# Two of three row blocks direct, a third of the pairs partly through products of transformed rows: a 3x3 convolution with group normalisation

## Chip, core and metric

One core of one Trainium2 chip. The metric is the device time of one execution in microseconds, the median of several runs. Five engines work in parallel, each in the order of its own queue: TensorE (PE, with its weight loads PEld), VectorE (DVE), ScalarE (ACT), GpSimd (POOL) and SyncE (SP), which issues all DMA transfers here. They are ordered against each other by semaphores alone.

## What is computed

```python
# x: 32 images of 64 channels, 56 x 56, float32; W: 64 x 64 x 3 x 3
bw = sign(W)                                   # value of clip(W) + (sign(W) - clip(W))
g = x.reshape(32, 32, 2, 56, 56)               # 32 groups of two channels
n = (g - mean(g)) / sqrt(var(g) + 1e-5)        # over the two channels and all pixels
out = x + conv(n.reshape(x.shape), bw, padding=1)
```

## The kernel before

Two images make a **pair**: their 2 x 64 channels fill the 128 partitions. There are 16 pairs. A pair's x lies in one of eight slots of `xbuf` and receives the result in place. x is normalised (times 512) into an upper half and a lower half, both float16, in `halves`; the products of both with the signs are summed in float32.

**TensorE** (L388 to L447) works in four quadrants of 64 x 64. Two of them, "home", put an image's rows into the PSUM partitions of its own image; the other two, "away", put them into the other image's partitions. A phase has 7 rows of each stream: first nine taps on the upper half, then nine on the lower. One tap of one stream is a *step* of two matmuls. A pair has four phases, two per group of 28 rows, and a PSUM bank for each block; banks alternate by group, so that group e waits until the results of group e-2 have been taken out. Before its nine lower taps a phase waits for POOL's lower half of the rows that it reads (`wait_lower`). Before the first pair, 14 rounds of matmuls on constants (L393) run while the data arrive, then the weights are turned by matmuls (L401) and copied out of PSUM by ACT (L272, L273).

**DVE** (L291 to L386), for pair k: adds the home rows of the group before to x (`add_home`, L345), takes seven statistics of pair k+2 (`pair_stats`, L302), adds home and away rows of the pair's first group (L345, L353), then makes the coefficients of pair k+2 (`coefficients`, L304 to L324), in which ACT takes a square root.

**ACT** (L236 to L289), for pair k: moves the away rows of the second group of pair k-2 out of PSUM (`move_away`, L268), waits for the coefficients of k, writes upper halves and the float32 normalised values by chunks of rows (L258, L250), takes the square root for k+1 (L245).

**POOL** (L205 to L234), for pair k: adds the rows that ACT moved for pair k-2 to x (`add_away`, L225), then subtracts upper halves from the normalised values to make the lower halves, chunk by chunk (`lo`, L216). Pairs 0 and 1 have four chunks, later ones two (rows 0 to 28 and 29 to 55). POOL and ACT thus prepare pair k while TensorE computes pair k-1.

**SP** (L160 to L203) stores a group once its home and away rows are added, and loads pieces of pair k+4 as phases of pair k end.

## Time and profile before

| | us |
|---|---|
| median of 3 runs | 209.88 (209.35 to 210.86) |
| the profiled execution | 210.1 |
| its span, first to last instruction | 208.3 |
| busy in the span: PE, DVE, ACT, POOL | 197.3, 154.3, 136.4, 128.4 |

The profile is one execution. Its page gives busy times, a chain of work followed back from the last instruction, and groups of instructions by line. The trace behind it gives instructions in order of time, with what ended the idle time before them. Durations of matmuls are modelled at their ends; their starts and the waits of other engines for them show TensorE's pace.

### The profile page before, as it was taken

To read this page: it belongs to the slowest core of one execution; us is meant where nothing else is said; L and a number is where in the kernel's file an instruction comes from. 1 tells how busy PE (TensorE), PEld (TensorE's weight loads), DVE (VectorE), ACT (ScalarE), POOL (GpSimd) and SP (SyncE) were. 2 spreads that over 40 slices of the span, in tenths; PEclk is the share of its full clock that TensorE was granted. 3 is DMA by queue.
4 is the path that set the end of the run, shared out by engine and by line. 5 is a ranking of instruction groups with operands and counts; after the bars stand their busy time and mean duration, and the time that the engine had idled before them with its cause. 6 is when DMAs were issued, how large, how long until landed. Compare 5 with 4: busy or idle time off the path is not lost.

```text
span 208.3 us, 10333 instructions
## 1 busy us (share of the span) xinstructions
PE 197.3 (95%) x4754; PEld 178.2 (86%) x4754; DVE 154.3 (74%) x317; ACT 136.4 (65%) x122; POOL 128.4 (62%) x56
## 2 busy tenths in 40 slices
PE   0979999999999999999999999999999999999990
PEld 0568898989898898989888898989888999999990
DVE  1897999987777887777778887777778787534092
ACT  3187979784939486693939587593939678492100
POOL 1026867975775939575784948576693957577300
PEclk9979999999999999999999999999999999999999
DMA  6999657999696967979686968968696334434345
GB/s 223 366 401 358 227 163 235 342 309 335 216 323 227 312 200 266 340 232 344 231 321 220 318 223 301 321 230 311 235 318 208 146 116 157 159 157 157 129 150 190
DMA packets 18699, 52.19 MB, mean 251 GB/s; under 512 B 2080, under 2 KB 4384, under 8 KB 18656
## 3 DMA queue, kind: packets, MB, share of 16 engines
q1 hardware_dynamic: 18656, 51.54, 69.9%
q8 instruction: 37, 0.61, 1.1%
q14 instruction: 6, 0.05, 0.1%
HBM read 25.84 MB, written 25.69 MB: 247 GB/s over the span
## 4 chain that ended last, share of the span: by engine, by line
PE 92%; DVE 3%; DMA 2%; ACT 1%; issue 0%; DVEq 0%
PE psum L444 89%; PE psum L395 3%; DMA xbuf<-in_x_dram 2%; DVE xbuf L365 1%; DVE xbuf L353 1%; DVE xbuf L345 0%; PE psum L401 0%; DVE xbuf L361 0%; ACT halves L258 0%; ACT w_taps L272 0%; DVEq L95 0%; ACT w_taps L273 0%
## 5 line engine op out<-in xcount | busy, mean ns | idle before, releaser
L444 PE MATMUL psum<-halves,w_taps 64*64 64x385 f16 (+5 forms) x4680 | 191.1, 324 | 1.5 <-ACT halves L258 1.5
L444 PEld LDWEIGHTS psum<-halves,w_taps 64*64 64x64 f16 x4680 | 174.6, 108 | 17.9 <-ACT w_taps L273 1.6
L216 POOL TENSOR_TENSOR halves<-xnorm,halves 128x1624 f16<-128x1624 f32 (+4 forms) x35 | 100.0, 2872 | 37.1 <-ACT xnorm L250 36.8
L302 DVE BATCH_NORM_STATS2 stats<-xbuf 128x6 f32<-128x448 f32 x112 | 60.6, 613 | 3.7 <-DMA xbuf<-in_x_dram 3.6
L345 DVE SCALAR_TENSOR_TENSOR xbuf<-psum,xbuf 128x784 f32<-128x784 f32 x31 | 30.2, 974 | 38.2 <-PE psum L444 38.2
L258 ACT ACTIVATE halves<-xbuf,coef 128x1624 f16<-128x1624 f32 (+5 forms) x36 | 55.1, 1534 | 1.3 <-DVE coef L323 1.0
L250 ACT ACTIVATE xnorm<-xbuf,coef 128x1624 f32<-128x1624 f32 (+4 forms) x35 | 54.2, 1549 | 0.0
L225 POOL TENSOR_TENSOR xbuf<-xbuf,moved 128x784 f32<-128x784 f32 x15 | 27.9, 1860 | 29.1 <-ACT moved L268 29.1
L268 ACT ACTIVATE moved<-psum 64x784 f32<-64x784 f32 x30 | 24.6, 819 | 25.0 <-PE psum L444 24.6
L353 DVE SCALAR_TENSOR_TENSOR xbuf<-psum,xbuf 64x784 f32<-64x784 f32 x32 | 31.1, 973 | 1.0
L245 ACT ACTIVATE std<-own,eps 128x1 f32<-128x1 f32 x16 | 4.7, 295 | 22.6 <-DVE own L312 22.6
L395 PE MATMUL psum<-filler 64*64 64x448 f16 x56 | 5.3, 565 | 4.7 <-DMA xbuf<-in_x_dram 4.7
L312 DVE BATCH_NORM_AGGREGATE own<-stats 128x2 f32<-128x84 f32 x16 | 8.5, 534 | 0.6
L395 PEld LDWEIGHTS psum<-filler 64*64 64x64 f16 x56 | 2.4, 168 | 7.0 <-DMA xbuf<-in_x_dram 4.7
L241 ACT ACTIVATE w_sign<-w_raw 64x576 f16<-64x576 f32 x1 | 0.7, 682 | 6.4 <-DMA w_raw<-in_L_conv_W_dram 6.4
L319 DVE TENSOR_SCALAR dev<-var,inv,std 128x1 f32<-128x1 f32 x16 | 4.4, 273 | 0.6
L317 DVE RECIPROCAL inv<-std 128x1 f32<-128x1 f32 x16 | 2.6, 164 | 2.8 <-ACT std L245 2.8
L323 DVE TENSOR_SCALAR coef<-own,coef 128x1 f32<-128x1 f32 x16 | 3.4, 214 | 0.6
L309 DVE STREAM_SHUFFLE stats<-stats 128x42 f32<-128x42 f32 x16 | 3.2, 203 | 0.5
L321 DVE RECIPROCAL coef<-dev 128x1 f32<-128x1 f32 x16 | 2.6, 164 | 0.5
L314 DVE TENSOR_SCALAR var<-own 128x1 f32<-128x1 f32 x16 | 2.5, 154 | 0.6
L365 DVE SCALAR_TENSOR_TENSOR xbuf<-psum,xbuf 64x392 f32<-64x392 f32 (+2 forms) x6 | 2.6, 427 | 0.2
(19 smaller groups left out, 9.6 us busy)
## 6 DMA issues: line engine op xcount, KB each, us to landing
out_dram<-xbuf SPq DMA_DIRECT2D x63, 392.0 KB, 3.3
xbuf<-in_x_dram SPq DMA_DIRECT2D x48, 448.0 KB, 5.4
xbuf<-in_x_dram SPq DMA_DIRECT2D x16, 224.0 KB, 4.6
out_dram<-xbuf SPq DMA_DIRECT2D x1, 224.0 KB, 2.7
out_dram<-xbuf SPq DMA_DIRECT2D x1, 168.0 KB, 3.0
w_raw<-in_L_conv_W_dram SPq DMA_DIRECT2D x1, 144.0 KB, 6.1
```

The costliest lines, as they stand in the source:

```text
L216: nc.gpsimd.tensor_tensor(at(halves[:, k % HRING, 1, :], a, b), at(xnorm[:, k % NRING, :], a, b), at(halves[:, k % HRING, 0, :], a, b), AL ...
L225: nc.gpsimd.tensor_tensor(away, away, moved[:, m % 2], ALU.add).then_inc(add_done, 1)
L245: nc.scalar.activation(std[:], own[:, 1:2], ACT.Sqrt, bias=eps[:], scale=QUARTER).then_inc(std_ready, 1)
L250: nc.scalar.activation(at(xnorm[:, k % NRING, :], a, b), at(xbuf[:, s, :], a, b), ACT.Identity, bias=coef[:, s, 1:2], scale=coef[:, s, 0:1 ...
L258: nc.scalar.activation(at(halves[:, k % HRING, 0, :], a, b), at(xbuf[:, s, :], a, b), ACT.Identity, bias=coef[:, s, 1:2], scale=coef[:, s, ...
L268: nc.scalar.mul(moved[here, m % 2], psum[there, bank:bank + 2, 0:BN], 1.0 / SCALE).then_inc(move_done, 1)
L302: nc.vector.bn_stats(stats[:, n, :], xbuf[:, s, a:b]).then_inc(blocks_ready, 1)
L312: nc.vector.bn_aggr(own[:], stats[:]).then_inc(var_ready, 1)
L345: nc.vector.scalar_tensor_tensor(rows, psum[:, bank:bank + 2, 0:BN], 1.0 / SCALE, rows, ALU.mult, ALU.add).then_inc(home_done, 1)
L353: nc.vector.scalar_tensor_tensor(rows[here], psum[there, bank:bank + 2, 0:BN], 1.0 / SCALE, rows[here], ALU.mult, ALU.add).then_inc(away_d ...
L395: pe.matmul(psum[cols, 3 + 4 * (n // 2), 0:448], filler[lanes, 0:CO], filler[lanes, :], start=True, stop=True)
L444: mm = pe.matmul(outs[:, r0 - first:r1 - first, left:right], w_taps[lanes, t, :], ins[:, :, left + dx:right + dx], start=(half == 0 and n ...
```

## The change

In five of the sixteen pairs (2, 5, 8, 11, 14) the home stream computes rows 25 to 42, nine pairs of rows, through four products per two rows in place of six: from the rows above, odd, even and below, POOL makes differences and sums of x (`make_lines`: STEP = even - odd, DIFF of rows two apart, SUM = odd + even), ACT and DVE make their upper and lower halves (`line_upper`, `line_lower`, and POOL's `lo_sums`), and TensorE multiplies each of the four (9 x 56 = 504 columns) by three weights, sums and differences of the taps, that POOL makes once (`weights_of_products`). The first two products are scaled and combined with x by DVE (`turn`), added and subtracted by POOL (`cross`), and added to the last two by DVE into `xbuf` (`finish`). The other 13 home rows and 25 away rows of such a pair stay direct, in blocks of 7 and 6, and of 8, 8 and 9 rows. Both away units of such a pair are moved by ACT and added by POOL (before, DVE added the first). The lower and upper halves of rows 26 to 41 are not made for them.

Home and away have separate counters of finished blocks, and TensorE's order is made step by step: the stream with fewer columns so far goes next. The chain of coefficients is cut into `aggregate`, at the end of DVE's round, and `scale`, at the start of the next, with a third coefficient for the sums. At the start there are 11 rounds on constants instead of 14 and 7 more after the weights are turned; the weights are copied out in three parts, two of them after the first upper half.

```diff
 AHEAD = 4
-WARM_UP = 14
+WARM_UP = 11
+KEEP_WARM = 7
+
+
+
+
+
+WINOGRAD = (2, 5, 8, 11, 14)
...
+    WROW, WROWS = 25, 18
+    WPAIRS = WROWS // 2
+    WN = WPAIRS * W
+
+    def home_units(k):
+        if k == LAST:
+            return [[(0, 7), (14, 7)], [(28, 7), (42, 4)], [(50, 3)]]
+        if k in WINOGRAD:
+            return [[(WROW + WROWS, 7), (WROW + WROWS + 7, 6)], [2, 1], [0, 3]]
+        return [[(0, 7), (14, 7)], [(28, 7), (42, 7)]]
+
+    def away_units(k):
+        if k == LAST:
+            return [[(7, 7), (21, 7)], [(35, 7), (46, 4)], [(53, 3)]]
+        if k in WINOGRAD:
+            return [[(0, 8), (8, 8)], [(16, 9)]]
+        return [[(7, 7), (21, 7)], [(35, 7), (49, 7)]]
...
+    def by_scalar(k, i):
+
+        return k != LAST and (i == 1 or k in WINOGRAD)
...
+        if k in WINOGRAD:
+            return [(0, 26), (42, 56)]
...
+            def store_unit(k, i):
+                if k in WINOGRAD:
+                    if i == 0:
+                        wait_away(k, 0)
+                        store(k, 0, 16)
+                        sp.wait_ge(home_done, home_before(k) + 1)
+                        store(k, WROW + WROWS, H)
+                    else:
+                        wait_away(k, 1)
+                        store(k, 16, WROW)
+                        sp.wait_ge(home_done, home_before(k) + 3)
+                        store(k, WROW, WROW + WROWS)
+                    return
...
+                        sp.wait_ge(away_conv, away_blocks_before(k) + min(n, 3))
...
+            def make_lines(k):
+                s = k % XRING
+                for n in (1, 2):
+                    pool.wait_ge(loaded[s][n], landed(k))
+                if winograd_before(k):
+
+                    before = WINOGRAD[winograd_before(k) - 1]
+                    pool.wait_ge(home_done, home_before(before) + 2)
+                    pool.wait_ge(line_lo_ready, winograd_before(k))
+                    pool.wait_ge(sums_norm_ready, winograd_before(k))
+                pairs_of_rows = at(xbuf[:, s, :], WROW, WROW + WROWS).rearrange("p (r m) -> p r m", m=2 * W)
+                odd, even = pairs_of_rows[:, :, 0:W], pairs_of_rows[:, :, W:]
+                nc.gpsimd.tensor_tensor(lines[:, STEP].rearrange("p (r w) -> p r w", w=W), even, odd,
+                                        ALU.subtract).then_inc(lines_made, 1)
+                nc.gpsimd.tensor_tensor(lines[:, DIFF], at(xbuf[:, s, :], WROW - 1, WROW + WROWS - 1),
+                                        at(xbuf[:, s, :], WROW + 1, WROW + WROWS + 1), ALU.subtract).then_inc(lines_made, 1)
+                nc.gpsimd.tensor_tensor(lines[:, SUM].rearrange("p (r w) -> p r w", w=W), odd, even,
+                                        ALU.add).then_inc(lines_made, 1)
...
+            def lo_sums(k):
+                n = winograd_before(k)
+                pool.wait_ge(sums_norm_ready, n + 1)
+                pool.wait_ge(line_hi_ready, 2 * (n + 1))
+                nc.gpsimd.tensor_tensor(line_halves[:, 1, SUM], sums_norm[:], line_halves[:, 0, SUM],
+                                        ALU.subtract).then_inc(sums_lo_ready, 1)
+
+            def cross(k):
+                n = winograd_before(k)
...
+                nc.gpsimd.tensor_tensor(crossings[:, 0], turns[:, 0], turns[:, 1], ALU.add).then_inc(crossed, 1)
+                nc.gpsimd.tensor_tensor(crossings[:, 1], turns[:, 0], turns[:, 1], ALU.subtract).then_inc(crossed, 1)
+
+            def weights_of_products():
+                pool.wait_ge(w_ready, KH)
+                middle, above, below = (w_taps[:, n] for n in range(KH))
+                nc.gpsimd.tensor_tensor(w_outer[:], above, below, ALU.add).then_inc(outer_ready, 1)
+                nc.gpsimd.tensor_scalar(w_products[:, 0], above, 1.0 / SCALE, 0.0, ALU.mult, ALU.add).then_inc(products_ready, 1)
+                nc.gpsimd.tensor_scalar(w_products[:, 3], below, -1.0 / SCALE, 0.0, ALU.mult, ALU.add).then_inc(products_ready, 1)
+                pool.wait_ge(outer_ready, 1)
+                nc.gpsimd.tensor_tensor(w_products[:, 1], w_outer[:], middle, ALU.add).then_inc(products_ready, 1)
+                nc.gpsimd.tensor_tensor(w_products[:, 2], w_outer[:], middle, ALU.subtract).then_inc(products_ready, 1)
...
             for k in range(NP):
 
                 if k >= 2:
-                    add_away(2 * (k - 2) + 1)
+                    if k - 2 in WINOGRAD:
+                        cross(k - 2)
+                    add_away(k - 2, 1)
+                if k in WINOGRAD:
+                    make_lines(k)
                 for c in range(len(chunks(k))):
                     if (k, c) != (0, 0):
                         lo(k, c)
-            add_away(LAST - 2)
+                if k in WINOGRAD:
+                    lo_sums(k)
+                if k - 1 in WINOGRAD:
+                    add_away(k - 1, 0)
+                if k == 1:
+                    weights_of_products()
+            if LAST - 1 in WINOGRAD:
+                cross(LAST - 1)
+            add_away(LAST - 1, 1)
...
+                unit = away_units(k)[i]
+                size = unit[0][1] * W
                 for here, there in ((LOW, HIGH), (HIGH, LOW)):
-                    nc.scalar.mul(moved[here, m % 2], psum[there, bank:bank + 2, 0:BN], 1.0 / SCALE).then_inc(move_done, 1)
+                    nc.scalar.mul(moved[here, m % 2, 0:len(unit) * size].rearrange("p (n m) -> p n m", m=size),
+                                  psum[there, bank:bank + len(unit), 0:size], 1.0 / SCALE).then_inc(move_done, 1)
...
+            def line_upper(k):
...
+                act.wait_ge(lines_made, 3 * n + 2)
...
+                nc.scalar.activation(line_halves[:, 0, 0:3 * WN], lines[:, 0:3 * WN], ACT.Identity,
+                                     scale=coef[:, s, 0:1]).then_inc(line_hi_ready, 1)
+                act.wait_ge(lines_made, 3 * n + 3)
...
+                                     bias=coef[:, s, 2:3], scale=coef[:, s, 0:1]).then_inc(line_hi_ready, 1)
...
+                nc.scalar.activation(sums_norm[:], lines[:, SUM], ACT.Identity,
+                                     bias=coef[:, s, 2:3], scale=coef[:, s, 0:1]).then_inc(sums_norm_ready, 1)
...
             act.wait_ge(w_turned, 1)
-            nc.scalar.copy(w_taps[:, 0:8, :], psum[:, 0, :].rearrange("p (t o) -> p t o", o=CO)).then_inc(w_ready, 1)
-            nc.scalar.copy(w_taps[:, 8, :], psum[:, 1, 0:CO]).then_inc(w_ready, 1)
+            w_copy(0)
...
+                    if (k, c) == (0, 0):
+                        w_copy(1)
+                        w_copy(2)
+                    else:
                         normalise(k, c)
+                if k in WINOGRAD:
+                    line_upper(k)
                 if k + 1 < NP:
                     deviation(k + 1)
-            move_away(LAST - 2)
+                if k - 1 in WINOGRAD:
+                    move_away(k - 1, 0)
+            move_away(LAST - 1, 1)
...
+            def scale(k):
...
+                nc.vector.tensor_scalar(coef[:, s, 2:3], own[:, 0:1], -2.0, coef[:, s, 0:1],
                                         ALU.mult, ALU.mult).then_inc(coef_ready, 1)
...
+                if k in WINOGRAD:
+                    (first, rows), (second, fewer) = home_units(k)[i]
+                    add_rows(k, bank, first, rows)
+                    add_rows(k, bank + 1, second, fewer).then_inc(home_done, 1)
+                    return
...
+            def line_lower(k):
+                n = winograd_before(k)
+                dve.wait_ge(line_hi_ready, 2 * n + 1)
...
+            def turn(k):
...
+                dve.wait_ge(home_conv, home_blocks_before(k, 1) + 1)
+                dve.wait_ge(lines_made, 3 * (n + 1))
+                nc.vector.scalar_tensor_tensor(turns[:, 1], psum[:, bank, 0:WN], 1.0 / SCALE, lines[:, STEP],
+                                               ALU.mult, ALU.subtract).then_inc(turned, 1)
+                dve.wait_ge(home_conv, home_blocks_before(k, 1) + 2)
+                nc.vector.scalar_tensor_tensor(turns[:, 0], psum[:, bank + 1, 0:WN], 1.0 / SCALE, lines[:, SUM],
                                                ALU.mult, ALU.add).then_inc(home_done, 1)
...
+            def finish(k):
...
+                dve.wait_ge(crossed, 2 * (n + 1))
+                dve.wait_ge(home_conv, home_blocks_before(k, 3))
+                for j in range(2):
+                    row = nc.vector.scalar_tensor_tensor(
+                        pairs_of_rows[:, :, j * W:(j + 1) * W], crossings[:, j].rearrange("p (r w) -> p r w", w=W), 0.5,
+                        psum[:, bank + j, 0:WN].rearrange("p (r w) -> p r w", w=W), ALU.mult, ALU.add)
+                row.then_inc(home_done, 1)
...
             for k in range(NP):
 
-                if k >= 1:
-                    add_home(2 * k - 1)
+                if 1 <= k < NP - 1:
+                    scale(k + 1)
+                if k >= 1 and k - 1 not in WINOGRAD:
+                    add_home(k - 1, 1)
                 if 1 <= k < NP - 2:
-                    pair_stats(k + 2)
-                add_home(2 * k)
-                add_away(2 * k)
+                    pair_stats(k + 2, range(4))
+                if k - 1 in WINOGRAD:
+                    finish(k - 1)
+                if 1 <= k < NP - 2:
+                    pair_stats(k + 2, range(4, NSTAT))
+                add_home(k, 0)
+                if k not in WINOGRAD:
+                    add_away(k, 0)
                 if k == 0:
-                    pair_stats(2)
+                    pair_stats(2, range(NSTAT))
                 if k < NP - 2:
-                    coefficients(k + 2)
-            for n, p in enumerate(phases[phases_before(LAST):]):
-                add_phase(p, n)
+                    aggregate(k + 2)
+                if k + 1 in WINOGRAD:
+                    line_lower(k + 1)
+                if k in WINOGRAD:
+                    turn(k)
...
+            warm(KEEP_WARM)
...
+            def wait_bank(b):
+
+                if b.unit < 2:
+                    return
+                if not b.away:
+                    pe.wait_ge(home_done, b.unit - 1)
+                elif by_scalar(*AWAY[b.unit - 2]):
+                    pe.wait_ge(move_done, 2 * moves_before(b.unit - 1))
+                else:
+                    pe.wait_ge(away_done, 2 * aways_before(b.unit - 1))
...
+            def wait_lower(b):
+                k = b.pair
+                if b.product == 1:
+                    pe.wait_ge(sums_lo_ready, winograd_before(k) + 1)
+                elif b.product is not None:
+                    pe.wait_ge(line_lo_ready, winograd_before(k) + 1)
...
+            for k in range(NP):
+                home, away = blocks_of(k, False), blocks_of(k, True)
+
+                home_time = away_time = 0
+                h = a = home_step = away_step = 0
+                while h < len(home) or a < len(away):
+                    if h < len(home) and (a == len(away) or home_time <= away_time):
+                        step(home[h], home_step)
+                        home_time += columns(home[h])
+                        h, home_step = (h, home_step + 1) if home_step + 1 < 2 * home[h].halfway else (h + 1, 0)
+                    else:
+                        step(away[a], away_step)
+                        away_time += columns(away[a])
+                        a, away_step = (a, away_step + 1) if away_step + 1 < 2 * away[a].halfway else (a + 1, 0)
```

## Rows read from the trace of the kernel before

**Rows 1.** The page: busy time by engine; the chain's shares by line.

```profile
PE 197.3 (95%) x4754; PEld 178.2 (86%) x4754; DVE 154.3 (74%) x317; ACT 136.4 (65%) x122; POOL 128.4 (62%) x56
...
PE psum L444 89%; PE psum L395 3%; DMA xbuf<-in_x_dram 2%; DVE xbuf L365 1%; DVE xbuf L353 1%; DVE xbuf L345 0%; PE psum L401 0%; DVE xbuf L361 0%; ACT halves L258 0%; ACT w_taps L272 0%; DVEq L95 0%; ACT w_taps L273 0%
```

**Rows 2.** Timeline, one steady pair: start, duration (us), engine, line, operation, [idle before <-releaser].

```profile
85.30 0.97 DVE L345 SCALAR_TENSOR_TENSOR xbuf<-psum,xbuf 128x784 f32<-128x784 f32 x1 [0.77 <-PE psum L444]
85.30 1.66 ACT L268 ACTIVATE moved<-psum 64x784 f32<-64x784 f32 x2 [1.72 <-PE psum L444]
...
86.99 1.75 ACT L258 ACTIVATE halves<-xbuf,coef 128x1624 f16<-128x1624 f32 x1
87.04 1.87 POOL L225 TENSOR_TENSOR xbuf<-xbuf,moved 128x784 f32<-128x784 f32 x1 [2.11 <-ACT moved L268]
...
90.44 6.31 POOL L216 TENSOR_TENSOR halves<-xnorm,halves 128x1624 f16<-128x1624 f32 x2 [1.53 <-ACT xnorm L250]
91.28 0.98 DVE L345 SCALAR_TENSOR_TENSOR xbuf<-psum,xbuf 128x784 f32<-128x784 f32 x1 [1.31 <-PE psum L444]
91.81 1.63 ACT L250 ACTIVATE xnorm<-xbuf,coef 128x1512 f32<-128x1512 f32 x1
92.29 1.98 DVE L353 SCALAR_TENSOR_TENSOR xbuf<-psum,xbuf 64x784 f32<-64x784 f32 x2
...
95.11 0.15 DVE L314 TENSOR_SCALAR var<-own 128x1 f32<-128x1 f32 x1
...
96.14 0.21 DVE L323 TENSOR_SCALAR coef<-own,coef 128x1 f32<-128x1 f32 x1
97.12 1.67 ACT L268 ACTIVATE moved<-psum 64x784 f32<-64x784 f32 x2 [1.72 <-PE psum L444]
```

**Rows 3.** Groups by shape: line, engine, operation, shapes, count | busy us, mean ns.

```profile
L216 POOL TENSOR_TENSOR halves<-xnorm,halves 128x1624 f16<-128x1624 f32 x14 | 46.0, 3288 | 21.6 <-ACT xnorm L250 21.6
L216 POOL TENSOR_TENSOR halves<-xnorm,halves 128x784 f16<-128x784 f32 x4 | 6.7, 1680 | 13.4 <-ACT xnorm L250 13.3
L225 POOL TENSOR_TENSOR xbuf<-xbuf,moved 128x784 f32<-128x784 f32 x15 | 27.9, 1860 | 29.1 <-ACT moved L268 29.1
L209 POOL TENSOR_SCALAR_AFFINE_SELECT ident<-ident 64x64 f16<-64x64 f16 x1 | 0.2, 234 | 0.2 <-POOL ident L207 0.2
L337 DVE TENSOR_TENSOR halves<-xnorm,halves 128x840 f16<-128x840 f32 x1 | 1.0, 1034 | 0.3 <-ACT halves L258 0.3
L361 DVE SCALAR_TENSOR_TENSOR xbuf<-psum,xbuf 128x392 f32<-128x392 f32 x1 | 0.6, 567 | 0.0
```

**Rows 4.** Timeline, columns as before: the startup, pair 2's preparation, the last pair.

```profile
12.46 1.03 DVE L337 TENSOR_TENSOR halves<-xnorm,halves 128x840 f16<-128x840 f32 x1 [0.30 <-ACT halves L258]
12.46 9.85 PE L444 MATMUL psum<-halves,w_taps 64*64 64x392 f16 x193 [1.50 <-ACT halves L258]
14.30 1.68 POOL L216 TENSOR_TENSOR halves<-xnorm,halves 128x784 f16<-128x784 f32 x1 [12.95 <-ACT xnorm L250]
...
25.19 3.34 POOL L216 TENSOR_TENSOR halves<-xnorm,halves 128x784 f16<-128x784 f32 x2 [0.18 <-ACT xnorm L250]
...
33.47 6.32 POOL L216 TENSOR_TENSOR halves<-xnorm,halves 128x1624 f16<-128x1624 f32 x2 [1.54 <-ACT xnorm L250]
...
38.02 1.66 ACT L268 ACTIVATE moved<-psum 64x784 f32<-64x784 f32 x2 [0.17 <-PE psum L444]
...
197.66 0.98 DVE L345 SCALAR_TENSOR_TENSOR xbuf<-psum,xbuf 128x784 f32<-128x784 f32 x1 [4.94 <-PE psum L444]
```

**Rows 5.** Windows, TensorE: stretch, length, busy (instructions), granted clock, DMA.

```profile
11.00:12.40 1.40, 0.00 (x0) 1.00 1.05 406
13.00:13.50 0.50, 0.50 (x14) 0.62 1.10 430
13.50:16.00 2.50, 2.50 (x38) 0.50 1.02 396
16.00:17.00 1.00, 1.00 (x26) 0.74 1.04 404
```

More of the change, by code:

```diff
@@ L53, in conv_preact_kernel @@
     NP = B // 2
-    LAST = 2 * NP - 1
-    phases = []
-    for e in range(2 * NP):
-        first = 28 * (e % 2)
-        here = 2 * (e % 2)
-        if e < LAST:
-            cuts = [(first, 7, here), (first + 14, 7, here + 1)]
-        else:
-            cuts = [(first, 7, here), (first + 14, 4, here + 1), (first + 22, 3, (here + 2) % 4)]
-        phases += [Phase(e // 2, e, row, n, bank, 4 + bank) for row, n, bank in cuts]
-    def phases_before(e):
-        return 2 * e + (e > LAST)
-    def by_scalar(e):
-        return e % 2 == 1 and e != LAST
@@ new lines, in away_blocks_before, with blocks_of @@
+    def away_blocks_before(k, i=0):
+        return (sum(len(u) for j in range(k) for u in away_units(j))
+                + sum(len(u) for u in away_units(k)[:i]) if k < NP else sum(len(u) for j in range(k) for u in away_units(j)))
+    def blocks_of(k, away):
+        out = []
+        for i, unit in enumerate(away_units(k) if away else home_units(k)):
+            u = (away_before(k) if away else home_before(k)) + i
+            for j, what in enumerate(unit):
+                bank = 2 * (u % 2) + j + (4 if away else 0)
+                if isinstance(what, int):
+                    out.append(Block(k, u, bank, away, WROW, WROWS, what))
+                else:
+                    out.append(Block(k, u, bank, away, *what))
+        return out
@@ L189, in _ @@
                 if k >= 1:
-                    store_group(2 * k - 1)
+                    store_unit(k - 1, 1)
                 if XRING <= k + AHEAD < NP:
@@ L356, in add_phase, with add_rows @@
[L356 to L366 removed]
+            def add_rows(k, bank, first, rows):
+                part = at(xbuf[:, k % XRING, :], first, first + rows)
+                return nc.vector.scalar_tensor_tensor(part, psum[:, bank, 0:rows * W], 1.0 / SCALE, part, ALU.mult, ALU.add)
@@ new lines, in add_last @@
+            def add_last(n, home, away):
+                dve.wait_ge(home_conv, home_blocks_before(LAST, 1) + n + 1)
+                add_rows(LAST, home.bank, home.first, home.rows).then_inc(home_done, 1)
+                dve.wait_ge(away_conv, away_blocks_before(LAST, 1) + n + 1)
+                part = at(xbuf[:, LAST % XRING, :], away.first, away.first + away.rows)
+                for here, there in ((LOW, HIGH), (HIGH, LOW)):
+                    nc.vector.scalar_tensor_tensor(part[here], psum[there, away.bank, 0:away.rows * W], 1.0 / SCALE,
+                                                   part[here], ALU.mult, ALU.add).then_inc(away_done, 1)
@@ L368, in _ @@
             for k in range(2):
-                pair_stats(k)
-                coefficients(k)
+                pair_stats(k, range(NSTAT))
+                aggregate(k)
+                scale(k)
                 if k == 0:
@@ new lines, in _, with last_chunk @@
+            mm.then_inc(w_turned, 1)
+            warm(KEEP_WARM)
[6 more added lines that the diff above has]
+                    pe.wait_ge(move_done, 2 * moves_before(b.unit - 1))
+                else:
+                    pe.wait_ge(away_done, 2 * aways_before(b.unit - 1))
+            def last_chunk(b):
+                k = b.pair
+                return next(n for n, (a, z) in enumerate(chunks(k)) if min(b.first + b.rows, H - 1) < z)
```

301 lines of the change are left out of this document (191 added, 110 removed).

## The prediction

> **What bounds the kernel now.** I read the page first. TensorE is busy 95% of the span and one matmul line is 89% of the chain that ended last; every other engine is below 75% [rows 1]. So time is made or lost on TensorE only, and the question is which other engine would become late for it. The timeline of one steady pair answers that [rows 2]. A pair takes 97.12 - 85.30 = 11.82 us, its first half 91.28 - 85.30 = 5.98 us for 36 steps (18 taps for each of two blocks), 166 ns a step; the second half takes 5.84 us. The 0.14 us between them are the six steps in which one stream lacks the image's edge row: each of the two streams (home, away) goes at its own pace, and a step is priced by its columns: 392 cost 166 ns, so 336 cost 142, 448 cost 190, 504 cost 214.
>
> Write T for the moment at which a pair starts on TensorE (85.30). Then ACT moves the last away rows from T to T+1.7, writes the next pair's halves, and its last normalised chunk ends at T+8.1 (91.81 + 1.63). POOL adds the moved rows T+1.7 to T+3.6, idles, starts the next pair's lower halves at T+5.14 and is done at T+11.45, with only 0.4 us of the pair left. DVE's last coefficient is ready at T+11.05. POOL is nominally 62% busy, but its work lies late in the pair: that is the engine to watch.
>
> **Startup before.** The pair of index 2 starts at 38.0 (ACT's move, released by TensorE) and POOL's halves for it run 33.47 to 39.8 [rows 4]. TensorE stood still from 11.0 to 12.4; its granted clock then fell to 0.5, the lower of its two levels (1.2 of 2.4 GHz), from about 13.1 to 16.5 by the fractions 0.62 and 0.74 [rows 5]: 3.4 us at half, 1.7 us lost.
>
> **The change: TensorE.** In pairs 2, 5, 8, 11, 14 ("W pairs") the home stream has 24 steps of 504 columns (5.13 us), 18 of 392 (2.99) and 18 of 336 (2.56), less 0.14 at the edge: 10.54 us. Away: 36 of 448 (6.83), less 0.14, and 18 of 504 (3.85): 10.54 us. A W pair saves 11.82 - 10.54 = 1.28 us; five save **6.4 us**. All else must be hidden to keep it.
>
> **Prices on POOL.** Its lower halves cost 3.288 us for 1624 elements, 1.680 for 784; its add of two f32 operands 1.860 for 784, so 2.37 ns an element [rows 3]. The new operations are such adds; I take 2.37, with 2.02 (3288/1624) as the low end. make_lines has 2016 elements: 4.78 us (low 4.07). cross has 1008: 2.39 (2.04). The add of 896 moved elements: 2.13 (1.81). Chunks of 1456 and 784: 2.97 between the two measured sizes, and 1.68; lo_sums 1.08. The five weight operations of 192 f16 elements: 0.46 each, 2.3 (low, by the 0.234 of a 64x64 operation: 1.2; high, on the line through the lower halves: 2.7).
>
> **First W pair (pair 2).** Before, POOL finishes pair 1's halves at 25.19 + 3.34 = 28.53 [rows 4]. The third coefficient adds one 0.21 us instruction before them: 28.8. Then in POOL's queue: weights 2.3, pair 0's add 1.86 (its move ends before that), make_lines 4.78, the two chunks 4.65: **42.4** (low 40.6, high 42.8). TensorE may start pair 2 by 36.1, two pairs after 12.4, but reaches the lower half of its first block after 9 steps, 1.5 us, and stands until 42.4. All of it is thus as late as if it had started at 40.9: **+2.9 us** against 38.0 (1.1 to 3.3). The longer fill, the weights copied in three parts and the earlier start are worth nothing to the end, since POOL's chain, not TensorE's, sets 42.4; that chain starts at the coefficients. If the wait were gone, they would bring up to 2 us.
>
> Standing still for some 4.8 us costs clock: 1.4 us did before. I take the same **+1.7 us** (0.5 to 2.5, as the trace has this event once).
>
> **Later W pairs, their start.** POOL, from T-11.82: add until T-8.21, lines until T-3.43, chunks until T+1.22, needed at T+1.5: 0, with 0.3 us of cover. ACT's three line_upper operations (1512, 504, 504 elements; 1624 take 1.75) fit between its last chunk at T-5.2 and T-1.6. line_lower is one DVE instruction, 1.8 us by the 1.034 of the 840-element one; it runs after the aggregate (which ends 95.26 in the steady pair, so here T-1.86), T-1.86 to T. Behind it stands scale, which gives coefficients at T+1.1, while ACT asks for them at T+1.7: 0.
>
> **Later W pairs, their end.** ACT moves the 16 away rows at T+8.4 to T+10.3, and TensorE wants their bank at T+10.54: 0, cover 0.2. POOL finishes the next pair's halves at T+11.45 as before, then adds 896 (T+13.6), and only then crosses (T+16.0). DVE's finish is two instructions of 504, 0.68 each between 0.567 and 0.97: T+17.4. TensorE needs that bank when the next pair's second home unit starts, T+10.54+5.9 = T+16.45. It stands 0.9 us (low 0.25, high 1.1), in-order, so both streams wait. Behind finish on DVE wait three statistics, three adds and the aggregate, some 5.5 us, done at about T+23 when the pair ends at T+23.3: no second stall. In pair 2 POOL has no idle before the halves, since ACT ran ahead, and the cross comes in time. Four stalls: **+3.6 us** (1.0 to 4.4).
>
> **Queues.** SP's stores of a W pair now wait for POOL's adds at T+13.6 and T+17.2, and two loads behind each; they fetch four pairs ahead, over 20 us early: 0. The tail: DVE's add at 197.66 started as TensorE began the last pair's second half [rows 4]; now finish releases that half and the add follows, so the 10.6 us from there are unchanged.
>
> **Sum.** 2.9 + 1.7 + 3.6 - 6.4 = +1.8 us on the profiled execution's 210.1 (span 208.3 and 1.8 around it): 211.9. The median is 0.2 lower: **211.7**.
>
> **Rivals.** *DVE and POOL take turns.* line_lower is the only DVE instruction with both tensors in SBUF that meets a working POOL. The one such instruction of before, 1.03 us, ran with POOL idle (12.46 to 13.49, POOL's first halves at 14.30) [rows 3, 4], so no row excludes this. If it must wait for the running POOL operation and the next POOL operation for it, pair 2's second chunk comes 1.8 us later. In later W pairs line_lower runs from T-0.5 to T+1.3, the second chunk ends at T+3.0: 1.5 us of standing at T+1.5. What follows then counts from T+1.5, and POOL's idle before the next halves is gone (0.7 us), which leaves 0.2 of the 0.9 at finish: +0.8 each. 1.8 + 4 x 0.8 = 5.0: **216.7**. The Trainium skill, SBUF — State Buffer, section "Who interferes with whom", says that a VectorE instruction with two SBUF inputs contends with a GpSimd instruction that reads SBUF, and that the one that issues second blocks until the first is done. By that rule the time would be the 216.7; no run here shows it yet.
>
> *POOL is cheap (other side).* At 2.02 ns an element and 0.234 us for each weight operation: pair 2 +1.1, clock +1.7, four stalls of 0.25: 3.8 - 6.4 = -2.6: **207.3**. For it: the larger lower halves do go at 2.02. Against: the only all-f32 row is 2.37. Each 0.1 ns is worth about 1.0 us (lines 0.2, four times 0.19 for add and cross); it decides for "not slower" at 2.19 ns.
>
> *Steps run in lockstep.* If a short step waited for the long one beside it, 36 steps would go at 190 and 24 at 214 ns: 11.9 us, nothing saved: 218.2. Against: the 5.84 us half.
>
> **Chances.** Forecast 0.42; taking turns 0.38; cheap POOL 0.15; lockstep or a DVE that loses every turn to POOL 0.05. The range 208.3 to 217 leaves out the better half of cheap POOL and the last case; the forecast's own is 209 to 214. Over 1% (some 2.1 us, about what a measurement of this kernel can tell) faster: 0.11, from cheap POOL and a little of the forecast. Slower: 0.61, from taking turns, the last case and somewhat under half of the forecast. Within: 0.28.
>
> **What would show it.** Three pairs' period 2 x 11.82 + 10.54 + 0.9 = 35.1 us instead of 35.5; TensorE idle from about 37.6 to 42.4, released by POOL's lower half, then a granted clock of 0.5; an idle of 0.9 us released by finish in pairs 6, 9, 12, 15; POOL without idle from 28.8. Taking turns would show as line_lower starting, or seeming to last, until POOL's first chunk ends, and the second chunk behind it. I am wrong if make_lines takes under 4 us, if TensorE idles elsewhere, or if W pairs don't take 10.5 us of matmuls.

## The result

| | us |
|---|---|
| before, same chip, median of 7 | 209.88 (209.19 to 211.66) |
| after, median of 7 | 215.69 (214.95 to 218.70) |
| ratio after / before | 1.0255, 95% interval 1.0214 to 1.0296 |
| predicted | 211.7 (208.3 to 217.0) |

The change costs 5.8 us (4.5 to 6.2 by the interval) where 1.8 was forecast. The time lies in the range, near the rival "DVE and POOL take turns" (216.7). The profiled execution of after is the slowest of its seven (218.7, span 216.9), so its second pair is read beside other kernels below. The page of after, busy time and the chain by engine and by line; it answers to [rows 1]:

```profile
PE 194.4 (90%) x4470; PEld 169.7 (78%) x4470; DVE 172.8 (80%) x348; ACT 149.8 (69%) x148; POOL 175.7 (81%) x96
...
PE 41%; POOL 22%; ACT 13%; issue 12%; DVE 7%; DMA 3%; SPq 1%; DVEq 0%; ACTq 0%; POOLq 0%
PE psum L732 41%; POOL halves L314 10%; ACT halves L419 7%; DVE line_halves L578 4%; ACT xnorm L411 4%; DMA w_raw<-in_L_conv_W_dram 3%; POOL lines L345 3%; POOL lines L343 3%; POOL lines L347 2%; POOL xbuf L329 2%; DVE xbuf L570 1%; SPq L237 1%; ACT line_halves L442 1%; DVE xbuf L539 1%; DVE xbuf L605 1%
```

TensorE works 2.9 us less than before (194.4 against 197.3) in a longer span, and only 41% of the chain is its own, where one line of it had 89% before: other engines now set when it goes on. For whom it waits, the waits of TensorE in after say (waited for: us in total, times, longest):

```profile
PE psum L732 <- POOL halves L314: 8.4, 5, 3.7
PE psum L647 <- DMA xbuf<-in_x_dram: 4.5, 1, 4.5
PE psum L732 <- DVE xbuf L539: 1.8, 1, 1.8
...
PE psum L732 <- DVE xbuf L605: 0.9, 1, 0.9
```

L314 is POOL's `lo`: one wait of 3.7 us in pair 2, and 4.7 us in four more, one per later pair with products ("W pair", as in the prediction). L605 is `finish`, for which four waits were forecast; there is one. The groups by shape of after (count | busy us, mean ns) stand against the prices drawn from [rows 3]:

```profile
L345 POOL TENSOR_TENSOR lines<-xbuf 128x1008 f32<-128x1008 f32 x5 | 11.7, 2346 | 0.0
L343 POOL TENSOR_TENSOR lines<-xbuf 128x504 f32<-128x504 f32 x5 | 6.4, 1274 | 0.0
L329 POOL TENSOR_TENSOR xbuf<-xbuf,moved 128x896 f32<-128x896 f32 x5 | 10.5, 2094 | 0.0
L314 POOL TENSOR_TENSOR halves<-xnorm,halves 128x1456 f16<-128x1456 f32 x5 | 14.8, 2967 | 0.0
L578 DVE SCALAR_TENSOR_TENSOR line_halves<-lines,coef,line_halves 128x1512 f16<-128x1512 f32 x5 | 21.1, 4225 | 1.0 <-ACT line_halves L442 1.0
```

POOL's operations cost what the prediction took: 2.35 us for 1008 elements, 2.09 for 896, 2.97 for 1456 (2.39, 2.13 and 2.97 forecast). One row is out of all proportion: DVE's `line_lower` (L578), priced at 1.8 us, lasts 4.2 us on average. The timeline of a later W pair in after (pair 5) shows why; POOL and DVE at the same time, then TensorE:

```profile
77.74 6.10 POOL L314 TENSOR_TENSOR halves<-xnorm,halves 128x1456 f16<-128x1456 f32 x2
...
79.18 3.13 DVE L578 SCALAR_TENSOR_TENSOR line_halves<-lines,coef,line_halves 128x1512 f16<-128x1512 f32 x1
...
83.90 4.29 PE L732 MATMUL psum<-halves,w_taps 64*64 64x392 f16 x98 [1.20 <-POOL halves L314]
```

POOL's first chunk (2.97 us) ends at 80.7. DVE's instruction, issued at 79.18, ends 1.6 us after that, at 82.3. POOL's second chunk ends at 83.84: the two chunks take 6.10 us, 1.45 more than the 2.97 + 1.68 of the prediction. Each has waited for the other, and TensorE stands 1.20 us.

### The profile page after: what moved, and what is told of

The parts are those of the page before. It is cut to its first block, busy times and chain, and to the rows that moved or that the text cites. A ratio compares the mean times of both kernels' runs of the same rounds, so it can differ in the third digit from the quotient of the medians.

```text
span 216.9 us, 9974 instructions
## 1 busy us (share of the span) xinstructions
PE 194.4 (90%) x4470; PEld 169.7 (78%) x4470; DVE 172.8 (80%) x348; ACT 149.8 (69%) x148; POOL 175.7 (81%) x96
## 4 chain that ended last, share of the span: by engine, by line
PE 41%; POOL 22%; ACT 13%; issue 12%; DVE 7%; DMA 3%; SPq 1%; DVEq 0%; ACTq 0%; POOLq 0%
PE psum L732 41%; POOL halves L314 10%; ACT halves L419 7%; DVE line_halves L578 4%; ACT xnorm L411 4%; DMA w_raw<-in_L_conv_W_dram 3%; POOL lines L345 3%; POOL lines L343 3%; POOL lines L347 2%; POOL xbuf L329 2%; DVE xbuf L570 1%; SPq L237 1%; ACT line_halves L442 1%; DVE xbuf L539 1%; DVE xbuf L605 1%
## 5 line engine op out<-in xcount | busy, mean ns | idle before, releaser
L732 PE MATMUL psum<-halves,w_taps 64*64 64x385 f16 (+9 forms) x4140 | 187.6, 327 | 9.9 <-POOL halves L314 8.4
L732 PEld LDWEIGHTS psum<-halves,w_taps 64*64 64x64 f16 x4140 | 160.6, 108 | 25.9 <-POOL halves L314 10.3
L314 POOL TENSOR_TENSOR halves<-xnorm,halves 128x784 f16<-128x784 f32 (+5 forms) x35 | 97.4, 2801 | 21.9 <-ACT xnorm L411 21.6
L419 ACT ACTIVATE halves<-xbuf,coef 128x784 f16<-128x784 f32 (+6 forms) x36 | 51.4, 1429 | 9.1 <-DVE coef L519 8.9
L411 ACT ACTIVATE xnorm<-xbuf,coef 128x784 f32<-128x784 f32 (+5 forms) x35 | 50.5, 1443 | 0.0
L432 ACT ACTIVATE moved<-psum 64x784 f32<-64x784 f32 (+2 forms) x40 | 31.3, 783 | 15.0 <-PE psum L732 14.3
L329 POOL TENSOR_TENSOR xbuf<-xbuf,moved 128x784 f32<-128x784 f32 (+2 forms) x20 | 35.4, 1771 | 7.5 <-ACT moved L432 7.5
L732 PE MATMUL psum<-line_halves,w_products 64*64 64x495 f16 (+1 forms) x240 | 26.6, 373 | 2.2 <-DVE xbuf L539 1.8
L605 DVE SCALAR_TENSOR_TENSOR xbuf<-crossings,psum 128x504 f32<-128x504 f32 x10 | 6.4, 677 | 19.8 <-POOL crossings L364 19.8
L578 DVE SCALAR_TENSOR_TENSOR line_halves<-lines,coef,line_halves 128x1512 f16<-128x1512 f32 x5 | 21.1, 4225 | 1.0 <-ACT line_halves L442 1.0
L732 PEld LDWEIGHTS psum<-line_halves,w_products 64*64 64x64 f16 x240 | 13.1, 107 | 8.4 <-DVE xbuf L539 2.3
L345 POOL TENSOR_TENSOR lines<-xbuf 128x1008 f32<-128x1008 f32 x5 | 11.7, 2346 | 0.0
L539 DVE SCALAR_TENSOR_TENSOR xbuf<-psum,xbuf 128x392 f32<-128x392 f32 (+3 forms) x13 | 6.2, 507 | 4.8 <-PE psum L732 4.6
```

The lines of the kernel that those rows point to most:

```text
L314: nc.gpsimd.tensor_tensor(at(halves[:, k % HRING, 1, :], a, b), at(xnorm[:, k % NRING, :], a, b), at(halves[:, k % HRING, 0, :], a, b), AL ...
L329: nc.gpsimd.tensor_tensor(away, away, part, ALU.add).then_inc(add_done, 1)
L345: nc.gpsimd.tensor_tensor(lines[:, DIFF], at(xbuf[:, s, :], WROW - 1, WROW + WROWS - 1), at(xbuf[:, s, :], WROW + 1, WROW + WROWS + 1), AL ...
L411: nc.scalar.activation(at(xnorm[:, k % NRING, :], a, b), at(xbuf[:, s, :], a, b), ACT.Identity, bias=coef[:, s, 1:2], scale=coef[:, s, 0:1 ...
L419: nc.scalar.activation(at(halves[:, k % HRING, 0, :], a, b), at(xbuf[:, s, :], a, b), ACT.Identity, bias=coef[:, s, 1:2], scale=coef[:, s, ...
L432: nc.scalar.mul(moved[here, m % 2, 0:len(unit) * size].rearrange("p (n m) -> p n m", m=size), psum[there, bank:bank + len(unit), 0:size], ...
```

## The experiments

Theory A: `line_lower`, which reads two tensors in SBUF, and POOL's operations take turns; that, and not POOL's amount of work, is what the forecast lacks. Theory B is the rival that each expectation names. Differences below are between medians; before's own median was between 209.9 and 210.5 on these chips, and the intervals reach 0.7 to 1.4 us to either side. So a difference under about 1 us rests on the waits and starts in the profiles, not on the medians.

### The changed kernel once more

No edit.

> The changed kernel once more, for a second profile. Theory A (DVE's line_lower, with both tensors in SBUF, and POOL's operations take turns): line_lower again lasts well over the 1.6 us that its 1512 elements need in all five pairs, and the POOL operation behind it starts when it ends. Theory B (the excess over the forecast is POOL's longer chain ahead of pair 2 and the clock; line_lower only looks long): the chain ahead of pair 2 ends later than the 42.4 us of the forecast. Both expect about 215.7 us.

Measured: one execution, 217.24 us. Its timeline in pair 2:

```profile
36.45 6.08 POOL L314 TENSOR_TENSOR halves<-xnorm,halves 128x1456 f16<-128x1456 f32 x2
36.91 4.09 DVE L578 SCALAR_TENSOR_TENSOR line_halves<-lines,coef,line_halves 128x1512 f16<-128x1512 f32 x1 [1.00 <-ACT line_halves L442]
```

The same stretch of the first profile of after:

```profile
37.55 4.57 POOL L314 TENSOR_TENSOR halves<-xnorm,halves 128x1456 f16<-128x1456 f32 x2
...
37.99 8.62 DVE L578 SCALAR_TENSOR_TENSOR line_halves<-lines,coef,line_halves 128x1512 f16<-128x1512 f32 x1 [1.00 <-ACT line_halves L442]
...
42.08 1.14 POOL L354 TENSOR_TENSOR line_halves<-sums_norm,line_halves 128x504 f16<-128x504 f32 x1
43.18 1.85 POOL L329 TENSOR_TENSOR xbuf<-xbuf,moved 128x784 f32<-128x784 f32 x1
...
47.60 1.74 ACT L419 ACTIVATE halves<-xbuf,coef 128x1624 f16<-128x1624 f32 x1 [6.37 <-DVE coef L519]
```

In this second profile `line_lower` lasts 3.1 to 4.1 us in all five pairs, and POOL's chunks for pair 2 end at 42.53, only 0.1 behind the forecast's 42.4: for A, and against the later chain of B. The clock of B did cost more in this execution: 2.8 us at 1.2 GHz behind a wait of 5.01 us, where the first profile lost 1.7 behind 3.68. In pair 2 of this execution DVE lost a single turn and POOL paid 1.5 us. In the first, DVE waited behind four POOL operations, until POOL's queue paused at 45.03, and then took 1.6 us; `scale` stood behind it, so ACT idled 6.37 us for the coefficients of pair 3. TensorE's waits of 1.8 and 0.9 us for DVE (L539, L605) follow from it.

### No second SBUF tensor

```diff
+            nc.gpsimd.memset(line_halves[:, 1, 0:3 * WN], 0.0).then_inc(zero_ready, 1)
...
-                nc.vector.scalar_tensor_tensor(line_halves[:, 1, 0:3 * WN], lines[:, 0:3 * WN], coef[:, k % XRING, 0:1],
-                                               line_halves[:, 0, 0:3 * WN], ALU.mult, ALU.subtract).then_inc(line_lo_ready, 1)
+                dve.wait_ge(zero_ready, 1)
+                for j in range(3):
+                    part = nc.vector.bn_stats(spare[:, 3 * n + j, :], lines[:, j * STAT:(j + 1) * STAT])
+                part.then_inc(line_lo_ready, 1)
```

The lower halves of the first three lines are left out (POOL sets them to zero once, at the start); three statistics of 448 elements, with one tensor in SBUF each, take as long on DVE.

> line_lower is replaced by three statistics of 448 elements, DVE work of about the same length (3 x 0.54 = 1.6 us) with one tensor in SBUF; the lower halves of the first three lines are left out (zeros), so their values are not made. Theory A: the forecast's sum holds, 211.7 us, that is some 4 us under the changed kernel; POOL's second chunk of a product pair lasts 1.7 us again, and TensorE no longer waits at its first lower taps in pairs 5, 8, 11, 14 but 0.9 us at finish. Theory B: within 1 us of the changed kernel's 215.7.

Measured: 212.81 us, ratio 1.0136 (1.0068 to 1.0204). POOL and DVE in pair 5, by its timeline:

```profile
71.92 4.60 POOL L317 TENSOR_TENSOR halves<-xnorm,halves 128x1456 f16<-128x1456 f32 x2
...
73.62 1.68 DVE L583 BATCH_NORM_STATS2 spare<-lines 128x6 f32<-128x448 f32 x3
```

And TensorE's waits in the same kernel (L610 is `finish` here, L317 POOL's `lo`):

```profile
PE psum L737 <- DVE xbuf L610: 3.6, 4, 0.9
PE psum L737 <- POOL halves L317: 2.9, 1, 2.9
```

2.9 us come back. POOL's chunks run unbroken (4.60 us) beside 1.68 us of DVE, the four waits for them are gone, and in their place stand the forecast's own: 0.9 us for `finish`, four times. A is right, though its 211.7 is 1.1 us short: the 1.6 us of DVE time were not the price. The statistics also write far less than `line_lower` does, but the write is not what blocks: the same operation with one of its tensors in PSUM and its result in SBUF (L345 of before) takes 0.97 us with POOL idle, at 85.30, and 0.98 beside POOL's halves, at 91.28 [rows 2]. What is left is the second SBUF tensor.

### Without the second pair

```diff
-WINOGRAD = (2, 5, 8, 11, 14)
+WINOGRAD = (5, 8, 11, 14)
```

> Only the list of pairs is changed: 5, 8, 11, 14 instead of 2, 5, 8, 11, 14. The startup's chain on POOL then has no lines in it. Theory A: 4 x 1.28 saved, some 1.5 us of the earlier start and full clock kept, and about 1.4 us lost in each of the four pairs by taking turns: about 208.9 us. Theory B: the stalls of these pairs are only the 0.9 us of finish: 206.9 us.

Measured: 209.44 us, ratio 0.9962 (0.9922 to 1.0003), nearer to A. TensorE's waits, and the starts of pairs 6 and 9 by ACT's moves:

```profile
PE psum L732 <- POOL halves L314: 4.8, 4, 1.2
...
84.19 1.20 ACT L432 ACTIVATE moved<-psum 64x504 f32<-64x504 f32 x2 [1.27 <-PE psum L732]
119.92 1.20 ACT L432 ACTIVATE moved<-psum 64x504 f32<-64x504 f32 x2 [1.27 <-PE psum L732]
```

Three pairs, one of them a W pair, thus take 35.73 us with turns, where before they took 3 x 11.82 = 35.46: nothing is left of the saving of 1.28.

Both edits together, the four pairs and the statistics in place of `line_lower`:

> Both edits: pairs 5, 8, 11, 14 and the statistics in the place of line_lower (the same lower halves are left out). Theory A: 209.9 - 1.5 - 4 x 1.28 + 4 x 0.9 = 206.9 us, 2 us under the run with the list alone. Theory B: the same time as the run with the list alone, to 0.5 us.

Measured: 207.86 us, ratio 0.9924 (0.9888 to 0.9960), with the four waits of 0.9 us for `finish` and none for POOL: A again, 1.0 above its 206.9. By the medians the turns cost 1.6 us in four later pairs, 0.4 each, and so 2.9 - 1.6 = 1.3 in pair 2. The starts of pairs say nearly the same for the later ones: 35.73 us for three pairs in the kernel with the list alone, 35.39 in the first kernel without the second tensor (its starts are shown further down), so 0.34 each. Pair 2 as a W pair costs 5.0 us without turns (212.81 - 207.86) and 6.3 with them.

### No pair with products

```diff
-WINOGRAD = (2, 5, 8, 11, 14)
+WINOGRAD = ()
```

> No pair is worked as products; what is left of the change is the coefficient chain in two parts, the separate home and away streams of TensorE and the products' weights, which are made and not used. Theory A (the loss is in the pairs with products, by turns of DVE and POOL and by the late second pair): startup gains the 1.2 us that the start of pair 2 moved from 38.02 to 36.82 in the kernel whose first such pair is 5, nothing else changes: 208.7 us. Theory B (part of the loss is in the other edits, the streams or the chain): 209.9 us or more.

Measured: 208.62 us, ratio 0.9953 (0.9916 to 0.9989), as A has it: the other edits are worth 1.3 us (0.2 to 1.8 by the interval). The windows of TensorE over the stretches of [rows 5]:

```profile
11.00:12.40 1.40, 1.40 (x34) 1.00 1.06 408
13.00:13.50 0.50, 0.50 (x21) 1.00 1.06 416
13.50:16.00 2.50, 2.50 (x68) 1.00 1.04 399
16.00:17.00 1.00, 1.00 (x32) 1.00 1.01 400
```

TensorE stood still from 11.0 to 12.4 before; now it is busy there (the rounds behind the weights' turning are in the queue at that place), and the granted clock stays at 2.4 GHz where it fell to 1.2. The startup edits were not tried one by one.

### Only the second pair

```diff
-WINOGRAD = (2, 5, 8, 11, 14)
+WINOGRAD = (2,)
```

> Only pair 2 is worked as products. Theory A (the second pair carries the loss, since POOL reaches it late and DVE's turn comes on top): 208.6 us of the kernel without products, plus the 6.25 us by which the changed kernel lies above the one that begins with pair 5 (215.69 less 209.44): 214.9 us. Theory B (every pair with products loses about the same, 7.1 us over five): 208.6 + 1.4 = 210.0 us.

Measured: 215.53 us, ratio 1.0242 (1.0181 to 1.0304). One W pair costs as much as five: 6.9 us above the kernel without products, for A and against B. Its timeline in pair 2 (POOL's chunks, TensorE's wait for them, the pair's end by ACT's move):

```profile
37.12 6.06 POOL L314 TENSOR_TENSOR halves<-xnorm,halves 128x1456 f16<-128x1456 f32 x2
...
43.24 5.85 PE L732 MATMUL psum<-halves,w_taps 64*64 64x392 f16 x98 [4.99 <-POOL halves L314]
...
54.10 1.20 ACT L432 ACTIVATE moved<-psum 64x504 f32<-64x504 f32 x2 [1.27 <-PE psum L732]
```

Windows of TensorE in the same kernel (length, busy, granted clock):

```profile
43.00:44.00 1.00, 0.76 (x12) 0.52 0.06 23
44.00:45.00 1.00, 1.00 (x18) 0.50 0.00 0
45.00:46.00 1.00, 1.00 (x18) 0.50 0.06 16
46.00:47.00 1.00, 1.00 (x24) 0.78 0.00 0
```

TensorE idles 4.99 us until POOL's chunks end at 43.18, and then runs at half clock: 0.76 x 0.48 + 2 x 0.50 + 0.22 = 1.6 us lost. Pair 3 begins at 54.10, 4.3 us later than the 49.84 of before and 5.5 later than the 48.59 of the kernel without products. A's price of 6.3 is short by 0.6. Another 1.3 us of the 6.9 lie behind the last add (its start to the span's end: 4.6 us here, 3.3 without products, 4.2 before), in the last stores; why was not tried.

### The same instruction, one step later

```diff
                     add_home(k - 1, 1)
+                if k in WINOGRAD:
+                    line_lower(k)
...
-                if k + 1 in WINOGRAD:
-                    line_lower(k + 1)
```

> The changed kernel with five pairs, where DVE does the lower halves of the first three lines one step later, behind the coefficients of the next pair and the add of the rows before, and no longer ahead of them. The work and its turn with POOL stay. Theory A (the price was the turn's place: it held up POOL's chunks and the coefficients): POOL's two chunks run unbroken in about 4.6 us, pair 3 has its coefficients as in the kernel with one tensor in SBUF, 212.8 us, finish waits 0.9 us as there. Theory B (sharing SBUF costs the same wherever it falls): 215.7 us.

Measured: 213.66 us, ratio 1.0148 (1.0086 to 1.0210); `line_lower` takes 1.78 to 2.30 us. Pair 2, and TensorE's waits for `finish` in the whole run:

```profile
37.70 4.58 POOL L314 TENSOR_TENSOR halves<-xnorm,halves 128x1456 f16<-128x1456 f32 x2
42.23 2.64 POOL L354 TENSOR_TENSOR line_halves<-sums_norm,line_halves 128x504 f16<-128x504 f32 x1
...
41.58 2.29 DVE L578 SCALAR_TENSOR_TENSOR line_halves<-lines,coef,line_halves 128x1512 f16<-128x1512 f32 x1
...
PE psum L732 <- DVE xbuf L605: 4.5, 4, 1.2
```

The turn is still there, but it falls on `lo_sums` (2.64 us against 1.14), for which TensorE does not wait. 2.0 of the 2.9 us come back with the same work done. Of the 0.9 missing to A's 212.8, `finish` can be the cause, which was waited for 4.5 us in four instead of 3.6; but this profile also waits 3.7 us for pair 2's chunks, where the other waits 2.9. So the price of a turn depends on its place: against B.

### The lines earlier, away rows by DVE, and both

From here on with pairs 5, 8, 11 and 14. POOL makes the lines ahead of its add:

```diff
+                    if k in WINOGRAD:
+                        make_lines(k)
                     add_away(k - 2, 1)
-                if k in WINOGRAD:
-                    make_lines(k)
```

> Products in pairs 5, 8, 11 and 14, and POOL makes the lines before it adds the moved rows of the pair before the last, so 1.8 us earlier, in a gap that it has there. DVE still takes its turn of about 3 us with POOL, but POOL's chunks are then far enough ahead. Theory A: TensorE's four waits of 1.2 us for POOL's second chunk go, the waits of 0.9 us for finish come back as in the kernel without the turn: 208.2 us. Theory B (POOL has too much work in these pairs, wherever it stands): 209.4 us, with the waits for POOL as before, only at another operation.

Measured: 211.00 us, ratio 1.0050 (1.0016 to 1.0083), slower than the 209.44 without the edit. Both theories miss. The waits for POOL's chunks did go, but the time did not fall with them. POOL and DVE in pair 8, by the timeline:

```profile
102.97 4.62 POOL L314 TENSOR_TENSOR halves<-xnorm,halves 128x1456 f16<-128x1456 f32 x2
107.52 1.17 POOL L354 TENSOR_TENSOR line_halves<-sums_norm,line_halves 128x504 f16<-128x504 f32 x1
...
106.32 3.96 DVE L578 SCALAR_TENSOR_TENSOR line_halves<-lines,coef,line_halves 128x1512 f16<-128x1512 f32 x1
```

DVE now waits until `lo_sums` has ended at 108.69, the next pair's last coefficient comes 2.6 us after the pair's start (111.03, start 108.42) instead of 1.8 (109.77, start 107.99), and the delay reaches `finish` (waits of up to 1.1 us, three) and the move (0.6). Three pairs take 36.56 us here (pairs 7 and 10 start at 96.60 and 133.16), against 35.71 without the edit (96.17 and 131.88).

DVE adds the first away unit of a W pair from PSUM; ACT's move and POOL's add of it are gone:

```diff
-        return k != LAST and (i == 1 or k in WINOGRAD)
+        return k != LAST and i == 1
...
-                if k not in WINOGRAD:
-                    add_away(k, 0)
+                add_away(k, 0)
...
```

> Products in pairs 5, 8, 11 and 14, and DVE, not ACT and POOL, adds the first away unit of such a pair straight from PSUM (POOL has 2.1 us less to do before the cross, ACT 1.85, DVE about 2 more). Theory A: the four waits of 1.2 us stand ahead of this work and stay; finish has no wait there in any case: 209.4 us. Theory B (POOL's amount of work is the bound): the waits shrink with the 2.1 us, 205 to 207 us.

Measured: 212.03 us, ratio 1.0094 (1.0052 to 1.0135). The waits of 1.2 us stayed, as A says, but its 209.4 misses by 2.6: 2.1 us of waits for `turn` (L593) came on top, since DVE does its adds ahead of it. TensorE's waits:

```profile
PE psum L731 <- POOL halves L314: 4.8, 4, 1.2
...
PE psum L731 <- DVE turns L593: 2.1, 3, 0.7
```

Both edits, and the weights of the products in turn 2 of POOL's loop:

> Both edits together, and the weights of the products made in the loop's turn 2. Theory A: neither the waits of 1.2 us for POOL's second chunk nor those of 0.9 us for finish are left; four pairs bring 1.28 us each: 209.4 less 4.8 is 204.6 us. Theory B: each edit's own gain, if any, without the rest: 206 or more.

Measured: 206.73 us, ratio 0.9836 (0.9778 to 0.9893). A is right on the two waits, which are gone, and B on the time. What is left:

```profile
PE psum L731 <- DVE turns L593: 2.9, 3, 1.0
```

Each edit alone loses and together they win. The third, the place of the weights, was not tried alone; in the kernel with these four pairs and no other edit, which makes them in turn 1, TensorE waits for POOL in the W pairs alone.

### Two attempts at what is left

The lower halves one step later, a first away unit of 9 rows for DVE and a second of 16 for ACT and POOL, `turn` ahead of the aggregate:

```diff
-            return [[(0, 8), (8, 8)], [(16, 9)]]
+            return [[(0, 9)], [(9, 8), (17, 8)]]
...
+                if k in WINOGRAD:
+                    add_away(k, 0)
+                    add_home(k, 0)
+                    turn(k)
...
```

> Products in pairs 5, 8, 11 and 14; the lower halves one step later as in the kernel with that edit alone; the away rows as a unit of 9 rows, which DVE adds from PSUM, and one of 16 rows, which ACT and POOL take behind the cross (POOL loses one add of 1.27 us ahead of the cross); turn ahead of the aggregate; the products' weights in turn 2. Theory A: no wait for POOL's chunks (no turn there), none for finish (the cross comes earlier), none for turn: 208.6 less four times 1.28 is 203.5 us, with up to 1 us of small waits 203.5 to 204.5 us. Theory B: 206 us or more, as the edits before it gave.

Measured: 208.25 us, ratio 0.9898 (0.9847 to 0.9948), a miss of A by 3.8 us or more. The away add, now ahead of `add_home`, makes that late (L535), and TensorE waits for it; the rest of the miss was not traced:

```profile
PE psum L734 <- DVE xbuf L535: 2.7, 3, 0.9
```

In the kernel with both edits, `turn` alone ahead of the aggregate:

```diff
                 add_away(k, 0)
+                if k in WINOGRAD:
+                    turn(k)
...
                     line_lower(k + 1)
-                if k in WINOGRAD:
-                    turn(k)
```

> The kernel with both edits (lines before the add, the first away unit added by DVE, weights in turn 2), where DVE does turn ahead of the aggregate of the pair after next, not behind it. Theory A (each engine's wait is one term, and the term left is the 1.0 us in which TensorE's next pair waits for the bank that turn empties): turn ends 0.85 us earlier, three times, so 206.7 less 2.5 is 204.2 us, and the wait for turn shrinks to 0.1 to 0.2 us. Theory B (the end moves to another wait again, as it did with each edit alone): 206 us or more, and the profile names the new wait.

Measured: 205.87 us, ratio 0.9852 (0.9785 to 0.9919). The wait for `turn` has shrunk, and no other wait of TensorE's loop is left:

```profile
PE psum L731 <- DVE turns L593: 0.5, 2, 0.2
```

The waits are as A has them and B's new wait is not there, but the time is 1.7 us above A's 204.2. Of the expected 2.5 us, 0.9 came at the medians, which the intervals do not tell from nothing (1.6 in the profiled executions, 206.37 to 204.81). The kernel with both edits and this one are below before and the changed kernel, each by its whole interval.

## Why the prediction was wrong

**The step that failed** is "Later W pairs, their start", in its sentence on `line_lower`: 1.8 us on DVE, at a cost of 0. Its time was nearly right (about 1.6 us), its cost was not, and the same instruction is missing in "First W pair". The prediction had the mechanism, among the rivals, and left it out of the sum although by its own words no row excluded it. The runs price it: 2.9 us in all by the medians, 1.3 of it in pair 2 and 4 x 0.4 later.

**The rival's size** was 5.0. Pair 2: 1.8 foreseen, 1.3 by the medians. Later pairs: it had the second chunk end at T+3.0 and 1.5 us of standing, with 0.2 of `finish`'s 0.9 left, +0.8 each; measured, 1.2 us of standing and nothing of `finish`, 1.2 - 0.9 = 0.3 by the waits and 0.4 by the medians. That the rival's 216.7 lies within 1.0 us of the measured time is partly luck: its 5.0 is 2.1 too much, and the sum under it is 1.0 too small. The Trainium skill, *SBUF — State Buffer*, section "Who interferes with whom", has the rule: a VectorE instruction with two SBUF inputs contends with a GpSimd instruction that reads SBUF, and one with a single SBUF input, outside VectorE's two-port modes, does not. The trace agrees on both halves, 3.13 us for 1.6 us of work in the one case, three statistics in 1.68 us beside unbroken chunks in the other.

**"First W pair"** was right in mechanism and in size, as far as the spread between executions tells. POOL's two chunks end at 42.4 by the forecast. They start at 36.45 to 37.70, by the execution, and take 4.57 or 4.58 us where no turn falls on them and 6.06 or 6.08 where one does, so they end between 41.13 (36.56 + 4.57) and 43.18. The lower clock behind TensorE's wait cost 1.6 us in the kernel with pair 2 alone, for 1.7. Pair 3 was to begin 2.9 + 1.7 - 1.28 = 3.3 us late. Without a turn on the chunks it begins 2.0 late in one profile (51.83, no second tensor, against 49.84) and 3.5 in another (53.31, one step later); with a turn, in the kernel with pair 2 alone, 4.3.

**"The earlier start is worth nothing to the end"** was right here, and the condition behind it too: the kernel without products gains 1.3 us, and its pair 2 starts 1.3 earlier (36.75 for 38.02). It stays hidden in the changed kernel, since POOL's chain sets the start of pair 2.

**"Later W pairs, their end"** was right in its waits, but for a kernel without turns: 0.9 us, four times, and none in pair 2. With turns TensorE is late enough at the start for `finish` to be in time, but for one wait in each profile of after: in the pair after 2 in the first, and in the second in the pair after 5, where the chunks had not been waited for.

**"TensorE"**: a W pair was to take 10.54 us and the period of three 35.1. In the kernel without the second tensor, the starts of pairs 5, 6, 7 and 8 by ACT's moves:

```profile
75.68 1.66 ACT L435 ACTIVATE moved<-psum 64x784 f32<-64x784 f32 x2 [1.75 <-PE psum L737]
...
86.19 1.19 ACT L435 ACTIVATE moved<-psum 64x504 f32<-64x504 f32 x2 [0.31 <-PE psum L737]
99.25 1.66 ACT L435 ACTIVATE moved<-psum 64x784 f32<-64x784 f32 x2 [0.70 <-PE psum L737]
111.07 1.66 ACT L435 ACTIVATE moved<-psum 64x784 f32<-64x784 f32 x2 [1.53 <-PE psum L737]
```

10.51 us for the W pair: the saving is real, and neither lockstep nor a cheaper POOL played a part. The pair after it takes 13.06 where 11.82 + 0.9 was forecast, and the period is 35.39. So a stall of 0.9 us costs 1.24: TensorE is shown idle for 0.87 us there, and busy for 12.19 with the 296 matmuls that take 11.82 in the next pair. This is the second term that was too small, 4 x 0.34 = 1.4 us. Without turns the kernel lies at +2.8 us (1.4 to 4.3 by its interval) where the sum had +1.8, and these stalls are enough for the difference.

## What to carry to other kernels

A new instruction on an engine with time to spare is not free if it shares something with an engine that has none: price it with the other's operation under way, and put that into the sum unless a row excludes it. Its place in the queue decides the price: in five pairs the turns cost 2.9 us when they fell on the chunks for which TensorE stood, and some 0.9, no more than the medians can tell from nothing, when they fell on `lo_sums`. And when several waits are near each other, taking one away shows only the next; the gain came when two (chunks and `finish`) were gone together.

## What the runs showed of the hardware

- A waiting DVE instruction does not always get the next turn. The same 1.6 us of work lasted 3.13 us (behind one POOL operation), 3.96 (behind two, the second of them `lo_sums`) and 8.62 (behind four, until POOL paused); in pair 2 of the same kernel it was 4.09 in one execution and 8.62 in another. What decides it was not tried.
- Filling a gap of 1.4 us at the start went with a granted clock of 2.4 GHz where it had fallen to 1.2 and cost 1.7 us. What such a fall cost did not follow the length of the idle time before it: 1.4 us behind 2.90 (no second tensor), 1.7 behind 3.68 (one step later), 1.6 behind 4.99 (pair 2 alone), but 2.8 behind 5.01 in the second execution of after.
- A stall costs more than its idle time also at the full clock: 0.87 us of idle for `finish` made its pair 1.24 us longer, with a granted clock of 1.00 throughout.
